# Fused cross attention and mixture of low-rank experts: token transposes moved off TensorE in the mixture

## The reference, cut to what matters

```python
def _L0_xattn_ref(q, k, v, gamma):        # q = layernorm(x), k = v = ctx, heads split the rows
    qk = jnp.einsum('bhdq,bhdl->bhql', qh, kh) * scale
    sm = jax.nn.softmax(qk, axis=-1)
    ret = jnp.einsum('bhql,bhdl->bhdq', sm, vh)
    return gamma * ret.reshape(B, Dv, Lq)

def _L0_ffn_ref(x, U, V, W1, b1, W2, b2): # B, S, D, K, R = 4, 1024, 1024, 8, 64
    h = jax.nn.relu(jnp.einsum('bsd,de->bse', x, W1) + b1)
    alpha = jax.nn.softmax(jnp.einsum('bse,ek->bsk', h, W2) + b2, axis=-1)
    vx = jnp.einsum('krd,bsd->bskr', V, x)
    uvx = jnp.einsum('kdr,bskr->bskd', U, vx)
    return jnp.einsum('bsk,bskd->bsd', alpha, uvx)

x = x + _L0_xattn_ref(_layernorm(x), ctx, ctx, gamma)
x = x + _L0_ffn_ref(_layernorm(x), U, V, W1, b1, W2, b2)
```

## Time and profile before

| | |
|---|---|
| time, median of 3 runs | 1603.02 us (1600.58 to 1603.8) |
| the profiled execution's own time | 1601.68 us |
| its span, first to last instruction | 1599.7 us |
| TensorE busy | 1544.4 us (97%), 6496 matmuls |
| VectorE, ScalarE, GpSimd busy | 988.6, 764.9, 715.5 us |
[...]

### The profile page before, as it was taken

The page is one execution under the profiler, slowest core; times in us unless marked ns, Lnnn a source line. Parts: engine busy times, 40 slices in busy tenths (PEclk is TensorE's granted clock), DMA queues, the critical chain, the costliest instruction groups (busy, mean ns, idle before and its releaser), DMA issues.

```text
span 1599.7 us, 21681 instructions
## 1 busy us (share of the span) xinstructions
PE 1544.4 (97%) x6496; PEld 1162.3 (73%) x6496; DVE 988.6 (62%) x1290; ACT 764.9 (48%) x1222; POOL 715.5 (45%) x523
## 2 busy tenths in 40 slices
PE   5999999999999999999779999999999999999999
PEld 3676777777677677776457877878778787877877
DVE  7999999999999999998644333323243232433212
ACT  5877778777777877777533122121211212112120
POOL 3898899999899899988620000000000000000000
PEclk9999999999999999999889999999999999999999
DMA  5999999999999999999871210303113021120302
GB/s 161 301 292 299 311 302 315 320 294 315 321 298 305 312 300 318 311 298 285 263 267 37 96 63 20 133 5 105 52 39 118 0 105 52 58 99 0 105 0 79
DMA packets 124574, 294.22 MB, mean 184 GB/s; under 512 B 26752, under 2 KB 31872, under 8 KB 124544
## 3 DMA queue, kind: packets, MB, share of 16 engines
q1 hardware_dynamic: 98192, 230.13, 45.2%
q10 hardware_dynamic: 26352, 63.71, 11.2%
HBM read 125.87 MB, written 33.69 MB: 100 GB/s over the span
## 4 chain that ended last, share of the span: by engine, by line
PE 50%; SPq 22%; DVE 11%; issue 7%; DMA 5%; POOL 4%; ACT 1%; DVEq 0%; ACTq 0%; POOLq 0%
PE scores L967 22%; SPq L230 18%; PE scores L1010 11%; PE attended L1028 11%; DVE pb L623 6%; DMA pt<-pb 3%; DVE neg_max L614 3%; PE spare L1047 2%; POOL pt_lo L337 2%; SPq L236 1%; POOL q_lo L328 1%; SPq L242 1%; SPq L247 1%; DVE stats L628 1%; PE scores L982 1%
## 5 line engine op out<-in xcount | busy, mean ns | idle before, releaser
L337 POOL TENSOR_TENSOR pt_lo<-pt,pt_hi 128x512 fp32r<-128x512 f32 (+1 forms) x256 | 401.4, 1574 | 60.3 <-ACT pt_hi L412 59.8
L437 ACT ACTIVATE probs<-scores,neg_max 128x1024 f32<-128x1024 f32 x256 | 285.0, 1113 | 185.3 <-DVE neg_max L614 184.0
L623 DVE STREAM_TRANSPOSE pb<-probs 128x1024 f32<-128x1024 f32 x256 | 316.5, 1236 | 22.2 <-DMA pt<-pb 16.2
L614 DVE TENSOR_REDUCE neg_max<-scores 128x1 f32<-128x1024 f32 x256 | 309.8, 1210 | 30.0 <-PE scores L560 29.1
L892 POOL TENSOR_TENSOR rstd<-var_eps,minus_half 128x1 f32<-128x1 f32 x28 | 17.2, 613 | 609.5 <-DVE var_eps L1093 609.5
L560 PE MATMUL scores<-k_hi,q_hi 128*128 128x512 f32 x512 | 226.9, 524 | 31.5 <-ACT probs L437 21.7
L911 ACT ACTIVATE hidden<-scores,b_col 128x512 f32<-128x512 f32 x64 | 44.2, 690 | 351.2 <-PE scores L967 351.2
L967 PE MATMUL scores<-nt_hi,w_hi 128*128 128x512 f32 x512 | 200.9, 392 | 8.8 <-DVE w_lo L1118 8.8
L1105 DVE TENSOR_TENSOR ht_lo<-hidden,ht_hi 128x512 fp32r<-128x512 f32 x64 | 44.3, 692 | 262.0 <-ACT ht_hi L914 262.0
L967 PE MATMUL scores<-nt_lo,w_hi 128*128 128x512 f32 x512 | 200.2, 391 | 0.0
L967 PE MATMUL scores<-nt_hi,w_lo 128*128 128x512 f32 x512 | 200.0, 391 | 0.0
(11 more groups left out here) (95 smaller groups left out, 2603.0 us busy)
## 6 DMA issues: line engine op xcount, KB each, us to landing
pt<-pb SPq DMA_DIRECT2D x512, 256.0 KB, 5.4
gain_row<-gains SPq DMA_DIRECT2D x64, 256.0 KB, 5.2
x<-x_out SPq DMA_DIRECT2D x64, 256.0 KB, 5.1
first_n<-x SPq DMA_DIRECT2D x32, 512.0 KB, 3.6
result<-x SPq DMA_DIRECT2D x64, 256.0 KB, 3.9
out<-result SPq DMA_DIRECT2D x64, 256.0 KB, 2.0
x_res<-in_x ACTq DMA_DIRECT2D x61, 256.0 KB, 5.8
k_raw<-in_ctx ACTq DMA_DIRECT2D x30, 512.0 KB, 6.2
```

Of the source, the lines that this page charges most:

```text
L337: nc.gpsimd.tensor_tensor(pt_lo[2 * parity + half][:, :, keys, :], pt[2 * parity + half][:, :, keys, :], as_f32(hi[half][q][:]), ALU.subtr ...
L437: nc.scalar.activation(probs[j % 2][:], scores[j % 2][:], ACT.Exp, bias=neg_max[:, j:j + 1], accum_out=row_sum[b][:, j:j + 1]).then_inc(s_ ...
L614: nc.vector.tensor_reduce(neg_max[:, j:j + 1], scores[j % 2][:], AX_X, ALU.max, negate=True).then_inc(s_max, 1)
L623: nc.vector.transpose(pb[half][:, :, j % HALF, :], probs[j % 2][:]).then_inc(s_blocks, 1)
```

## The change: what it does

1. The next group's tokens are no longer transposed by TensorE. VectorE normalises in place (`x_in`), turns the tile in 32x32 blocks (`turn_squares`, one STREAM_TRANSPOSE of 128x1024 for each tile), and SP gathers each tile with four transfers of 128 KB (runs of 1 KB) into `nt_raw`, which lies in the same bytes as `nt_lo`. ScalarE copies `nt_hi`, GpSimd subtracts in place for `nt_lo`. Partitions then hold features in another order (feature in the square times four plus quarter), so the rows of W1 and V are reordered on the host in the same way (`turned_rows`), and the free dimension of `nt_hi` is [tile 4, quarter 4, block 8, 32]: a moving operand of 512 tokens is 16 runs of 32 elements. The gathers wait until all value products of the group are done, as `nt_raw` takes the place of `nt_lo`.
2. The value products are turned round: stationary V, moving tokens (still 24 matmuls of 512 columns for each of four blocks of 128 ranks), into four PSUM banks. The values come out with ranks on partitions and need no transpose.
3. For the gate alpha must then be wide: TensorE transposes alpha once a group (32 x 128), ScalarE copies it out, SP stores it to DRAM (`alphas`) and reads it back, each row broadcast over 64 partitions, two transfers for each of four blocks of ranks, the third and fourth block's only after the first and second gate have freed the buffer. VectorE multiplies.
4. The experts' first tile (k = 0) is issued in the order r = 0, 1, 2 of both halves and then r = 3 of both, each r with a wait for its low part.
5. In the attention's end `normalise_first` writes its elements in the new order of features (four elements apart), and the copies after `turn_first` write in the new layout.

```diff
+        def gather(g, k):
+            if k == 0:
+                sp.wait_ge(s_v, g * RB + RB)
+            sp.wait_ge(s_squares, g * GT + (k + 1))
+            for a in range(4):
+                sp.dma_start(nt_raw[:, k, a, :, :].rearrange("p k c -> p (k c)"),
+                             squares[k % 2][32 * a:32 * a + 32, :, :, :].rearrange("p g k c -> p g (k c)")
+                             ).then_inc(s_n_in[k], 16)
+        def store_alpha(g):
+            sp.wait_ge(s_at, g + 1)
+            sp.dma_start(alphas[bass.ts(g, E), :].rearrange("e (k p) -> k e p", k=GT), alpha_t[:]).then_inc(s_at_out, 16)
+        def spread_alpha(g, r):
+            if r == 0:
+                sp.wait_ge(s_at_out, g * 16 + 16)
+            elif r > 1:
+                sp.wait_ge(s_gated, g * RB + (r - 1))
+            for e in range(2):
+                sp.dma_start(alpha_wide[r % 2][64 * e:64 * e + 64, :],
+                             alphas[bass.ds(g * E + (2 * r + e), 1), :].rearrange("a n -> (a n)")
+                             .partition_broadcast(64)).then_inc(s_wide[r % 2], 16)
 # SP, order in a group
             for i in range(4):
                 load_residual(g, i)
+            store_alpha(g)
+            for r in range(RB):
+                spread_alpha(g, r)
+            if not last:
+                gather(g, 0)
+                gather(g, 1)
             store(g, 0)
             for i in range(1, 5):
+                if not last and i < 3:
+                    gather(g, i + 1)
                 store(g, i)
                 load_residual(g, i + 3)
 # GpSimd
+        def low_n(g, k):
+            pool.wait_ge(s_nhi, g * GT + (k + 1))
+            nc.gpsimd.tensor_tensor(nt_lo[:, k], nt_raw[:, k], as_f32(nt_hi[:, k]), ALU.subtract).then_inc(s_nlo, 1)
 # ScalarE
+        def high_gated(g, r):
+            act.wait_ge(s_gated, g * RB + (r + 1))
+            nc.scalar.activation(gt_hi[:, r, :], gated[:, r, :], ACT.Copy).then_inc(s_ghi, 1)
+        def high_n(g, k):
+            act.wait_ge(s_n_in[k], g * GATHERS + GATHERS)
+            nc.scalar.activation(nt_hi[:, k], nt_raw[:, k], ACT.Copy).then_inc(s_nhi, 1)
+            act.wait_ge(s_at_turn, g + 1)
+            nc.scalar.activation(alpha_t[:], lt_ps[0:GT * E, 0:P], ACT.Copy).then_inc(s_at, 1)
+            for r in range(RB):
+                high_gated(g, r)
+            if not last:
+                for k in range(GT):
+                    high_n(g, k)
 # TensorE
-                ins = mm(work[e % 2], w[:, k, cols[e]], n[:, k, :], start=(k == 0 and i == 0),
+                ins = mm(work[e % 2], w[:, k, cols[e]], n[:, :, :, k, :], start=(k == 0 and i == 0),
+        def turn_alpha(g):
+            pe.wait_ge(s_alpha, g + 1)
+            pe.transpose(lt_ps[0:GT * E, 0:P], alpha[:].rearrange("p k e -> p (k e)"), ident[:]).then_inc(s_at_turn, 1)
-                n, w = ((nt_hi, v_hi), (nt_hi, v_lo), (nt_lo, v_hi))[i]
-                ins = mm(work[k % 2], n[:, d, k * P:(k + 1) * P], w[:, d, :], start=(d == 0 and i == 0),
+                w, n = ((v_hi, nt_hi), (v_lo, nt_hi), (v_hi, nt_lo))[i]
+                ins = mm(value_ps[r], w[:, d, r * P:(r + 1) * P], n[:, :, :, d, :], start=(d == 0 and i == 0),
+                if k == 0 and c == 0 and i == 0:
+                    pe.wait_ge(s_glo, g * RB + (r + 1))
+            if k == 0:
+                order = [(c, r) for c in range(2) for r in range(RB - 1)] + [(c, RB - 1) for c in range(2)]
+            big = value_products(g, 1)
+            issue_all(big[:16])
+            turn_alpha(g)
+            issue_all(big[16:])
+            for r in range(2, RB):
+                issue_all(value_products(g, r))
             for k in range(GT):
-                issue_all(interleave(expert_products(g, k, gated_unit[k]), turns_at(f"u{k}"), 2, 1))
+                issue_all(expert_products(g, k))
 # VectorE, order in a group
+                if e in NORMALISED_AT and not last:        # (2, 3, 6, 7); statistics at (1, 2, 5, 6)
+                    normalise(g, NORMALISED_AT.index(e))
+                if e in SQUARES_AT and not last:           # (3, 4)
+                    turn_squares(g, SQUARES_AT.index(e), first)
                 low_hidden(g, e)
             softmax(g)
+            gate(g, 0)
+            gate(g, 1)
+            low_gated(g, 0)
+            low_gated(g, 1)
+            for r in range(2, RB):
+                gate(g, r)
+                low_gated(g, r)
+            for i in range(2 * GT):
+                add_residual(g, i)
+                if i < 2 and not last:
+                    turn_squares(g, i + 2, first)
```

More of the change, by code:

```diff
@@ L771, in mixture @@
     assert place.at <= shared["top_at"]
[L774 removed]
+    work, lt_ps, l_ps, y_ps = (shared[name] for name in ("work", "lt_ps", "l_ps", "y_ps"))
+    value_ps = shared["spare"] + work
     s_u_in = sem("s_u_in")
@@ L934, in slot @@
             nc.scalar.activation(e_logits[:], centred[:], ACT.Exp).then_inc(s_exp, 1)
-            for stage, units in units_of(last).items():
-                for number, what, k, c in units:
-                    if what == "n":
-                        used = g * GT + (k + 1)
-                    else:
-                        used = None if (first and k < 2) else g * GT + (k - 1)
-                    high_unit(g, number, what, k, c, used)
+            act.wait_ge(s_at_turn, g + 1)
[3 more added lines that the diff above has]
+            if not last:
+                for k in range(GT):
+                    high_n(g, k)
         act.wait_ge(shared["s_pre"], 16 * len(shared["loads"]))
@@ L1056, in slot @@
         def slot(g, first, last):
-            beside = units_of(last)
             for e in range(KB):
@@ L1060, in slot @@
                 issue_all(big[:12] + (router_products(g, e - 1) if e else []) + big[12:])
-            def turns_at(stage):
-                return [turn for unit in beside.get(stage, []) for turn in turn_unit(g, *unit)]
             big = value_products(g, 0)
@@ L1159, in slot @@
         def slot(g, first, last):
-            beside = units_of(last)
-            def turned_after(what, k):
-                number = max(n for units in beside.values() for n, w, tile, c in units if (w, tile) == (what, k))
-                return g * UNITS + (LEAD + number + 1)
-            def low_units(stage):
-                for unit in beside.get(stage, []):
-                    low_unit(g, *unit)
             for e in range(KB):
@@ L1280, in cross_attention_and_mixture @@
         shared["turned"] = [tile[:] for tile in spare]
+        shared["spare"] = [tile[:].rearrange("p k n -> p (k n)") for tile in spare]
         shared["work"] = [scores[1][:, half] for half in halves]
@@ L1284, in cross_attention_and_mixture @@
         shared["y_ps"] = [tile[:] for tile in attended]
-        parts = (attention(nc, sem, x, ctx, ctx_t, gamma, x1, scratch, shared), mixture(nc, sem, x1, shared, out))
+        parts = (attention(nc, sem, x, ctx, ctx_t, gamma, x1, scratch, shared), mixture(nc, sem, x1, alphas, shared, out))
         block = stack.enter_context(nc.Block())
```

185 lines of the change are left out of this document (77 added, 108 removed).

## The result

After: 1585.02 us, median of 4 runs (1583.42 to 1587.27), against 1603.02 us for the kernel before in the same job (three runs, 1600.58 to 1603.80; a fourth took 1935.23 us, a fifth longer, and is left out); ratio 0.9887, 95% interval 0.9873 to 0.9901. The kernel is 18 us faster, the forecast was 40 (1563.0, 1557 to 1580). The direction was right, the size was not, and the time lies 5 us above the range that was given. The profiled execution took 1583.42 us, 1581.6 of it span.

A forecast was written before the change was run, and what follows sets the result against it. TensorE, busy 97% of the span, was taken as the bound: 1601.68 - 42.6 (transposes gone) + 1.0 (alpha's transpose) + 1.6 (experts' order) = 1561.7, or 1563.0 on the median's scale; range 1557 to 1580.

The forecast's parts named there:

- What bounds the kernel: Mixture: TensorE is busy throughout, so every start-to-start distance on it counts in full, other engines only when late for it.
- The transposes: Mixture, TensorE: 352 transposes go, all on the path at 0.121 us each, 42.6 us saved; alpha's transposes add 1.0.
- Moving operands in 16 runs ... I take zero: Hidden and value stages, 288 matmuls a group: moving operands in 16 runs of 32 elements cost nothing extra.
- rival B: Hidden and value matmuls: the moving operand's 16 runs cost a cycle each, +16 us, 1579; chance 0.06.
- From below: nothing: Bound on the run price: matmuls with four runs of 128 elements show 393 ns against 392 for one run.
- Experts' order: Expert stage's first tile: TensorE stalls 0.2 us a group for VectorE's add, 1.6 us in all; bounds 0 to 4.
- Alpha's chain: Beside the value stage: alpha's way over DRAM to the gates costs 0, slack 2.2 us at block 2, 1.8 at block 3.
- rival C: Alpha's way over DRAM at the attention's latencies: 5.4 us late in each of 8 groups, 43 us, 1606; chance 0.06.
- The gathers: Beside the expert stage: issues of 0.55 us, landing in 3.0, last low part with slack 4 us; cost 0.
- Hidden stage: VectorE's added squares and normalisations fit where it was two thirds idle: cost 0, bound 1 us.
- Part 5: Attention's end: four normalisations writing in 16-byte steps may cost ScalarE 2.5 us; counted 0, as TensorE waits 8.8 us anyway.

The follow-up runs named there:

- experiment 2: Kernel before, without the 224 transposes of the next group's tokens and their copies and subtractions: 1575.15 us, ratio 0.9829.
- runs_and_order: Changed kernel with nt_hi in one run, nt_lo in four runs of 128, and the experts' first tile reordered: 1561.14 us, ratio 0.9722.
- experiment 1: Sweep of 48 matmuls alone, only the moving operand's pattern changed: 0.2267 us each with one run, 0.2369 with the changed kernel's pattern.
- experiment 5: Second sweep of 48 matmuls alone, varying step and start: 16 runs take 10.92 us at step 96, 11.36 at 64 or 128.
- experts_order: Changed kernel with the experts' first tile reordered so half 0 is finished by matmul 18 instead of 21: 1584.11 us, ratio 0.9867.
- experiment 6: Changed kernel with only the experts' first tile reordered, half 0 finished by matmul 18 instead of 21: 1584.11 us, groups 94.67 to 94.69 apart.
- experiment 4: Changed kernel with nt_hi in one run and nt_lo in four runs of 128, raw tiles one tile further on: 1563.08 us, ratio 0.9754.
- experiment 10: Changed kernel with its 16 short runs alternating between 128-byte halves, six transfers a tile instead of four: 1608.03 us, ratio 1.0033.
- experiment 8: Sweep of matmuls alone with weights moved 128 bytes: the fast run (0.2267 us) becomes 0.2323, the one started 32 elements on goes from 0.2323 to 0.2277.
- experiment 9: Kernel with nt_hi in one run and nt_lo in four, these and everything placed behind moved 128 bytes on: 1577.79 us, ratio 0.9848.
- experiment 3: Changed kernel with nt_hi laid out as one run of 512 tokens, nt_lo still in 16 runs: 1571.21 us, ratio 0.9807.

## Why the prediction was right or wrong

**What bounds the kernel: right.** TensorE's starts counted in full, before and after: a change of 0.0100 us in one matmul of 512 columns came out as 22 us.

**The transposes: right.** 42.6 us forecast at 0.121; 0.122 measured in experiment 2. `runs_and_order` has neither slow patterns nor a stall: 97.87 - 92.05 = 5.82 us a group for 48 transposes less one of alpha, where the forecast's terms make 5.7. Over seven such groups and the last (93.99 - 92.05 = 1.94) that is 42.7, forecast 41.6.

**"Moving operands in 16 runs ... I take zero, by the row that is the same engine and kind": this step failed.** The price is 0.0100 us a matmul in rows of like ones. It was rival B's, with 0.06 of the chances, and B's estimate of +16 us (one element's time a jump) was even of the right size; its explanation was not, as experiment 1 shows no price up to 8 runs (10.88 us a row, as for one run) and experiment 5 only 0.0008 us a matmul for 16 runs at a step of 96 (10.92). What misled is the row held against it: four runs of 128 at 393 ns against 392 for one (in the earlier trace rows the first line, L967, is the one run and the second, L582, the four; the heading has them the other way round) are of a fast kind: 4 runs took one run's 10.88 us at steps of 2048 elements (experiment 1, L78) and of 192, 256 and 1024 (experiment 5, L87, L89, L91). That it compared durations and not starts did no harm: the duration grew by 11 ns (403 for 392) where the starts grew by 10. "From below: nothing" was right, "I take zero" was not, when the trace had no run that short. B's own time, 1579, was short of 1585 as well, by its lower price and by the stall below. The size in the kernel: `experts_order` has groups of 94.69 and `runs_and_order` 92.05, which differ in the layout of `nt_hi`, `nt_lo` and the raw tiles alone: 2.64 us a group, 21.1 us in eight. That is 0.0092 for each of 288 matmuls: in the hidden stage a block with its two router products grew by 0.21 us (6.15 for 5.94 from start to start in the chains), 0.0088 a matmul, in the value stage by 0.0100.

**Experts' order: right in place, size off.** 0.42 us a group instead of 0.2 (experiment 6), within the bound of 0.5. The rows of TensorE show 0.50 from 1085.71 to 1086.21, so 0.27 of waiting; the rest lies in the starts behind the gap, which stand somewhat further apart (1086.21 to 1086.55 is 0.34).

**The sum of the misses** has three terms: 21.1 for the moving pattern; 8 x 0.42 - 1.6 = 1.8 for the stall; and 42.7 - 41.6 = 1.1 the other way, for the transposes. 21.1 + 1.8 - 1.1 = 21.8 us; measured less forecast is 1585.0 - 1563.0 = 22.0. That the second form of experiment 4 came out at the forecast's very 1563 is in part luck, as these last two misses nearly cancel.

**Alpha's chain: right, rival C did not come.** The transpose of alpha went out at T0 = 1067.11, 2.5 us after alpha was done at 1064.63. The store was slower to issue (0.75), and gate 0 ended at 1074.05, T0 + 6.9 for a forecast of 6.7. gt_lo of block 2 ended at 1079.72, T0 + 12.6 for 12.0, before TensorE asked for it. A block's two spreads took about 0.48 us each to issue where I had 0.354 and register work. Block 3's low part ended at 1082.76, T0 + 15.65 for 15.1. The latencies of the mixture, not of the attention, were the right rows: the spreads landed 2.8 us after their issue at the median, 4.0 at the most.

**The gathers: right, with less room.** An issue took 0.61 us at the median (0.55 to 1.40), a landing 2.6 at the median and 4.7 at the most. GpSimd's last low part, in order of time:

```profile
1098.62 2.40 POOL L935 TENSOR_TENSOR nt_lo<-nt_raw,nt_hi 128x1024 fp32r<-128x1024 f32 x1 [3.00 <-ACT nt_hi L968]
```

It ends at 1101.02, 1.7 us before the first matmul of the next hidden stage at 1102.70; forecast was 4. The residual loads were later than reckoned (VectorE waited up to 3.4 us for one), which VectorE's room took in. The 1.5 us a tile of experiment 10 used it up.

**Hidden stage: right, cost 0.** VectorE's squares took 1.237 us and waited for transfers 2.1 us in the whole kernel.

**Part 5: cost 0 was right, the price of the writes was not.** The four normalisations that write every fourth element took 2.25 us each instead of 1.23, which is 4 x 1.02 = 4.1 us more of ScalarE for the 2.5 that were held for the range:

```profile
L485 ACT ACTIVATE first_n<-first_n,first_shift,first_rstd 128x1024 f32<-128x1024 f32 x3 | 6.8, 2253 | 0.1
```

That this cost TensorE nothing is seen at ScalarE's first copy for the split of W1. It still waited 3.25 us for the load of W1, where it waited 5.02 before:

```profile
805.74 1.06 ACT L950 ACTIVATE w_hi<-w_raw 128x1024 fp32r<-128x1024 f32 x1 [3.25 <-DMA w_raw<-in_w]
```

TensorE then waited 7.0 us for VectorE's split, 8.8 before, and the first hidden stage began at 814.57 against 815.12.

**Places, and elements apart.** For the matmul's moving operand places 128 bytes apart have different prices: one run took 0.2323 us for 0.2267 with the weights 128 bytes on (experiment 8), and the kernel 1577.8 us for 1563.1 with the moving tiles and all behind them 128 bytes on (experiment 9). A row of 48 with every fourth element, 16 bytes apart, takes 22.14 us, with every second, 8 bytes apart, 21.70, with one run 10.88 (experiment 1). ScalarE's four-apart writes of part 5 are not free either: 2.25 us for 1.23.

**What stays open.** The rule of the halves orders the rows of like matmuls in which runs start at multiples of 128 bytes; it is a description of these rows (0.2267 to 0.2277 where it is kept, 0.2323 and more where it is not), and no run shows what in the chip causes it. These don't follow from it: that one element of shift costs 0.0100, 16 elements 0.0025 and 8 or 32 elements 0.0056 to 0.0067; that 32 runs (0.2400) and 64 runs (0.2798) in one half cost more than 16; the 0.2306 of one-run matmuls between short-run ones (experiment 3); the expert stage of experiment 9; the even and odd blocks of experiment 10.

## What to carry to other kernels

When TensorE is the bound, price a matmul by the distance of starts in a row of like ones, and treat a moving pattern that the trace does not hold as unpriced: a sweep of 48 matmuls a pattern measures it. The rows that cost what one run costs (10.88 to 10.92 us for 48) had 2, 4 or 8 runs, of 64 elements of 4 bytes or more, with steps of a multiple of 256 bytes, beginning in the same half of a 256-byte block as the weights. Lay moving operands out like that, and let a copy that has to be made anyway do the reordering; here the layout turned 18 us of gain into 40, and with the experts' order into 44. The rows of like matmuls gave the right price for a kernel whose matmuls all have one kind of pattern; between mixed ones (experiments 3 and 10) they did not, so the kernel has to be measured too. Changes of a few tenths of a us a group are read from the chain's starts, not from medians that scatter by 3 us.

## What the runs showed of the hardware that was not expected

- The address of a tile in SBUF is a price: with the moving tiles and all behind them 128 bytes further on, 14.7 us more for the kernel (1577.8 for 1563.1), 0.0056 us a matmul of 512 columns alone.
- 16 runs of 32 elements cost 0.2367 us at steps of 64, 128, 256 and 512 elements, and 0.2267 to 0.2275 at 96, 160, 224 and 288, with weights that begin in the same half.
- A moving operand of every second element takes 0.452 us, twice one run's.
- A matmul with one run starts the next one 0.2306 us later instead of 0.2267 when every third matmul around it has 16 runs of 32 elements.
- ScalarE's normalisation of 128x1024 takes 2.25 us instead of 1.23 when it writes every fourth element.
- An issue on SP took 0.35 us for a residual load, 0.48 for a spread row, 0.61 for a gather of 128 KB, 0.63 for one of 64 KB in 128-byte runs and 0.75 for alpha's store (medians): half the bytes in shorter runs are not quicker to issue.
